# Context stack ahead of staging, routing exponentials behind the tanh, adds a slot later: a cross-attention and expert block on one core

## The reference

```
def layernorm(x): ...                     # mean and variance over the last axis
# cross attention, 16 heads of 64; the rows of the second layernorm are queries
ln = layernorm(layernorm(x)) * g + b      # 512 rows for each batch
xn = layernorm(context) * g + b           # 32 rows for each batch
q, kv = ln @ Wq, concat([xn @ Wkv, ln @ Wkv])
sim  = (rmsnorm(q) * 64**-0.5) @ rmsnorm(k).T   # 512 x 544 for each head; mask on the 32
attn = softmax(sim);  a = (attn @ v) @ Wout + bout
x = x + tanh(g_xattn) * a
# experts: 8, of width 256; all are computed, the two best of each row are kept
p = softmax(layernorm(x) @ router);  w = softmax of the two largest, 0 elsewhere
y = sum over e of w[e] * ((silu(h @ gate[e]) * (h @ up[e])) @ down[e])
x = x + tanh(g_ffn) * y
```

## Time and profile before

| | |
|---|---|
| median of 3 runs | 346.26 us |
| the profiled execution | 347.66 us, its span 345.9 us |
| TensorE busy | 301.0 us, 87% of the span |
| DVE busy | 273.5 us, 79% |
| GpSimd busy | 268.0 us, 78% |
| ScalarE busy | 204.9 us, 59% |
| mean granted TensorE clock | 0.975 |
| DMA engines, mean share | q1 28.8% |

### The profile page before, as it was taken

One profiled execution on the slowest core, in us unless ns is written; L12 is line 12 of the kernel. 1 busy time (PEld: TensorE's weight loads), 2 busy tenths in 40 slices (PEclk: granted clock), 3 DMA queues, 4 the chain that ended last, 5 costly groups with the idle time before them and its releaser, 6 DMA issues.

```text
span 345.9 us, 8714 instructions
## 1 busy us (share of the span) xinstructions
PE 301.0 (87%) x3321; PEld 184.3 (53%) x3321; DVE 273.5 (79%) x515; ACT 204.9 (59%) x357; POOL 268.0 (78%) x203
## 2 busy tenths in 40 slices
PE   0566578789999999999999999999987898988992
PEld 0233243446555555555555656788764674654652
DVE  3898878958899899898988976955647885887994
ACT  2463746727756757665766656467662657554551
POOL 8689896866999999999989987565971475875562
PEclk9996969989999999999999999999999999999999
DMA  6505322810712614416307259450100000001001
GB/s 165 151 1 127 69 35 44 193 39 17 174 45 49 152 36 107 106 23 148 69 20 164 60 154 181 112 165 9 38 2 3 2 1 0 2 3 31 2 0 33
DMA packets 33708, 23.63 MB, mean 68 GB/s; under 512 B 10818, under 2 KB 33154, under 8 KB 33666
## 3 DMA queue, kind: packets, MB, share of 16 engines
q1 hardware_dynamic: 32722, 23.03, 28.8%
q10 hardware_dynamic: 944, 0.04, 0.2%
HBM read 5.87 MB, written 0.52 MB: 18 GB/s over the span
## 4 chain that ended last, share of the span: by engine, by line
PE 53%; POOL 16%; issue 11%; ACT 5%; DVE 5%; SPq 4%; DMA 4%; POOLq 0%; DVEq 0%; ACTq 0%
POOL p_lo L628 9%; PE big L1526 7%; PE big L1527 7%; PE o_ps L1362 5%; PE big L1381 5%; PE o_ps L1356 4%; PE o_ps L1357 4%; DMA pc_st<-pc_lo 3%; PE tv L1369 3%; POOL rms_r L492 3%; PE pj L1333 2%; PE pj L1292 2%; PE pj L1293 1%; PE pj L1294 1%; POOL x_sb L641 1%
## 5 line engine op out<-in xcount | busy, mean ns | idle before, releaser
L593 POOL TENSOR_TENSOR p_lo<-p 128x1024 f16<-128x1024 f32 x64 | 121.8, 1915 | 13.1 <-ACT p L792 13.1
L792 ACT ACTIVATE p<-big 128x1024 f32<-128x1024 f32 x64 | 65.6, 1025 | 48.9 <-PE big L1527 48.8
L991 DVE TENSOR_REDUCE nm_main<-big 128x2 f32<-128x1024 f32 x64 | 78.2, 1222 | 18.1 <-PE big L1381 17.3
L492 POOL TENSOR_TENSOR rms_r<-meansq,power 128x8 f32<-128x8 f32 x32 | 52.3, 1637 | 16.1 <-DVE meansq L965 16.1
L628 POOL TENSOR_TENSOR p_lo<-p,p_lo 128x512 f16<-128x512 f32 x32 | 37.0, 1158 | 25.9 <-ACT p_lo L865 25.9
L1526 PE MATMUL big<-w 128*128 128x512 f16 x128 | 48.8, 381 | 1.9 <-ACT p L792 1.6
L1527 PE MATMUL big<-w 68*128 68x512 f16 x128 | 48.7, 380 | 0.0
L1356 PE MATMUL o_ps<-v,p 128*128 128x65 f16 x512 | 40.7, 194 | 0.0
L1357 PE MATMUL o_ps<-v,p 128*128 128x64 f16 x512 | 40.6, 195 | 0.0
L1356 PEld LDWEIGHTS o_ps<-v,p 128*128 128x128 bf16 x512 | 35.9, 99 | 6.7 <-issue 3.6
L1357 PEld LDWEIGHTS o_ps<-v,p 128*128 128x128 bf16 x512 | 34.4, 98 | 3.2
(11 more groups left out here) (228 smaller groups left out, 715.6 us busy)
## 6 DMA issues: line engine op xcount, KB each, us to landing
w<-hl SPq DMA_DIRECT2D x32, 256.0 KB, 4.2
w<-hl SPq DMA_DIRECT2D x32, 128.0 KB, 3.7
pc_st<-pc_hi SPq DMA_DIRECT2D x64, 32.0 KB, 1.9
pc_st<-pc_lo SPq DMA_DIRECT2D x32, 32.0 KB, 1.9
hl<-n_kernel_gating_EDF_dram SPq DMA_DIRECT2D x1, 1024.0 KB, 6.5
hl<-L_ffn_kernel_up_EDF_dram SPq DMA_DIRECT2D x1, 1024.0 KB, 5.5
o_sb<-in_L_xattn_Wkv_dram SPq DMA_DIRECT2D x2, 384.0 KB, 7.2
x_sb<-in_x_dram SPq DMA_DIRECT2D x2, 256.0 KB, 3.7
```

What stands on the lines that cost most here:

```text
L492: nc.gpsimd.tensor_tensor(rms_r[:, tau % QT, :], meansq[:, tau % QT, :], power[:, 0:8], ALU.pow).then_inc(rr_ok, 1)
L593: nc.gpsimd.tensor_tensor(p_lo[m % NP][:, :], p[m % NP][:, :], p_hi[m % NP], ALU.subtract).then_inc(plo_ok, 1)
L792: nc.scalar.activation(p[n % NP][:, :], st_ps, ACT.Exp).then_inc(exp_ok, 1)
L991: nc.vector.tensor_reduce(nm_main[:, u % 2, 2 * c:2 * c + 2, q], s2_ps.rearrange("p (k n) -> p k n", k=2), AX_X, ALU.max, negate=True).the ...
```

## The change

- `W_AT`: the staging of unit 1 is issued in slot 2 rather than slot 0, so behind the stack of unit 0, which is issued in slot 1.
- ScalarE: in slot 1 the context exponentials come ahead of the exponential of slot 2, not behind it.
- GpSimd: `pc_lo` of unit 0 is made at the end of slot 1, not in slot 2 behind that slot's p_lo.
- The second entry's row scale: DVE in slot 2 rather than 0, ScalarE's four activations in slot 3 rather than 2.
- Experts: `route_exp` is issued a slot later, behind the tanh and ahead of the cast. GpSimd's add of `ys` is a slot later. Expert 2 is weighted by DVE, not ScalarE; counts of the semaphores follow (`weighted`).
- Output: the second batch goes out in two transfers of two row tiles each.

```diff
--- before.py
+++ after.py
@@ -226,7 +226,7 @@
         qk_at = {8 * u - 20 + 2 * t: QT * u + t for u in range(2, UNITS) for t in range(QT)}
         t_at = {8 * u - 18 + 2 * t: QT * u + t for u in range(2, UNITS) for t in range(QT)}
         v_at = {16 * w - 13 + 4 * t: QT * w + t for w in range(1, UNITS // 2) for t in range(QT)}
-        W_AT = {8 * u - 8 if u else FIRST: u for u in range(UNITS)}
+        W_AT = {(FIRST, 2)[u] if u < 2 else 8 * u - 8: u for u in range(UNITS)}
         cs_at = {8 * u - 4: u for u in range(UNITS)}
 
         LN1_AT = 2
@@ -351,8 +351,14 @@
                 return rt_ps[:, 5].rearrange("p t e -> p (t e)")[:, k * QT:(k + 1) * QT]
             return rs[b][:, k, :]
 
+        BY_ACT = (0, 4, 6)
+
         def weighted_by_dve(e):
-            return e % 2 == 1
+            return e not in BY_ACT
+
+        def weighted(e):
+
+            return len([k for k in range(e + 1) if weighted_by_dve(k) == weighted_by_dve(e)])
 
         block = ctx.enter_context(nc.Block())
 
@@ -453,13 +459,13 @@
             for n in range(FIRST, LAST):
                 slot(n)
             out_v = out.rearrange("b (t p) d -> p (b t) d", p=P)
-            for half in range(B):
-                if half == 0:
-                    sp.wait_ge(yp_ok, E)
-                else:
-                    sp.wait_ge(y_ok, E * QT)
-                sp.dma_start(out_v[:, half * QT:(half + 1) * QT, :], x1[:, half * QT:(half + 1) * QT, :]).then_inc(out_ok, 16)
-            sp.wait_ge(out_ok, 16 * B)
+            sp.wait_ge(yp_ok, E)
+            sp.dma_start(out_v[:, 0:QT, :], x1[:, 0:QT, :]).then_inc(out_ok, 16)
+
+            for first in (QT, QT + 2):
+                sp.wait_ge(y_ok, (E - 2) * QT + first + 2)
+                sp.dma_start(out_v[:, first:first + 2, :], x1[:, first:first + 2, :]).then_inc(out_ok, 16)
+            sp.wait_ge(out_ok, 16 * 3)
 
         @block.gpsimd
         def _(pool):
@@ -595,7 +601,7 @@
                 if n == 1:
 
                     inverse_rms(qk_at[0])
-                if n == 2 or n > 2 and n - 1 in cst_at:
+                if n - 1 in cst_at:
                     u = n // 8
                     pool.wait_ge(cexp_ok, u + 1)
 
@@ -628,20 +634,17 @@
                     nc.gpsimd.tensor_tensor(hid_lo[m % NH], hid[m % NH], hid_hi[m % NH], ALU.subtract).then_inc(hlo_ok, 1)
                 if n == Z_X - 1:
                     second_scale(1)
-                m = n - 3
+                m = n - 4
                 if is_xslot(m) and m % FC == FC - 1 and expert_of(m)[1] == 0:
                     e = expert_of(m)[0]
-                    if weighted_by_dve(e):
-                        pool.wait_ge(ysd_ok, e // 2 + 1)
-                    else:
-                        pool.wait_ge(ysa_ok, e // 2 + 1)
+                    pool.wait_ge(ysd_ok if weighted_by_dve(e) else ysa_ok, weighted(e))
                     if e == 0:
                         pool.wait_ge(x1_ok, QT)
                     need(pool, yp_ok, e)
                     nc.gpsimd.tensor_tensor(x1[:, 0:QT, :], x1[:, 0:QT, :], ys[e % 2].rearrange("p (t d) -> p t d", t=QT),
                                             ALU.add).then_inc(yp_ok, 1)
 
-            for n in range(XSLOTS + 4):
+            for n in range(XSLOTS + 5):
                 expert_slot(n)
 
         @block.scalar
@@ -794,8 +797,8 @@
             def slot(n):
                 if is_slot(n) and n - 1 not in AHEAD:
                     exponentials(n)
-                if n in AHEAD:
-                    exponentials(n + 1)
+                if n == 0:
+                    exponentials(1)
                 if n - 1 in cst_at:
                     u = cst_at[n - 1]
                     act.wait_ge(cst_ok, u + 1)
@@ -806,6 +809,8 @@
                     nc.scalar.activation(pc_hi[:, :], o_ps[0][:, :], ACT.Exp, bias=mask_c[:, batch(u):batch(u) + 1])
                     nc.scalar.activation(pc[:, :], o_ps[0][:, :], ACT.Exp,
                                          bias=mask_c[:, batch(u):batch(u) + 1]).then_inc(cexp_ok, 1)
+                if n == 1:
+                    exponentials(2)
                 if n in qk_at and n > FIRST:
                     squared(qk_at[n])
                 if n in t_at:
@@ -817,7 +822,7 @@
                     need(act, pv_ok, 16 * (w - 1))
                     nc.scalar.activation(V[w % 2][:, t, :, 0:DH], tv[:, :].rearrange("p (h d) -> p h d", d=DH), ACT.Copy,
                                          scale=V_SCALE).then_inc(vhi_ok, 1)
-                if n == LN1_AT:
+                if n == LN1_AT + 1:
                     act.wait_ge(ln1b_ok, 1)
                     for t in range(QT, T):
                         nc.scalar.activation(z[:, t, :], x_sb[:, t, :], ACT.Identity, scale=ln_s[:, t:t + 1],
@@ -858,6 +863,12 @@
                         act.wait_ge(pv_ok, SLOTS - NP + n + 1)
                     need(act, hlo_ok, n + 1 - NH)
                     nc.scalar.activation(hid[n % NH], scores[n % 2][:, 0:512], ACT.Tanh, scale=0.5).then_inc(th_ok, 1)
+
+                for b, at in enumerate((ROUTE_X0, ROUTE_X1)):
+                    if n - 1 in at and 0 in at[n - 1]:
+                        route_exp(b, 0)
+                    if n - 1 in at and 5 in at[n - 1]:
+                        route_exp(b, 1)
                 m = n - 1
                 if is_xslot(m):
                     act.wait_ge(hid_ok, m + 1)
@@ -881,11 +892,6 @@
                         last = nc.scalar.activation(ys[e % 2][:, k * D:(k + 1) * D], o_ps[e % 2][:, k * D:(k + 1) * D],
                                                     ACT.Copy, scale=w_tok[:, k, e:e + 1])
                     last.then_inc(ysa_ok, 1)
-                for b, at in enumerate((ROUTE_X0, ROUTE_X1)):
-                    if n in at and 0 in at[n]:
-                        route_exp(b, 0)
-                    if n in at and 5 in at[n]:
-                        route_exp(b, 1)
 
             for n in range(XSLOTS + 4):
                 expert_slot(n)
@@ -1198,7 +1204,7 @@
                                                    in0=st_ps[0:BC, :].rearrange("p (h d) -> p h d", d=DH),
                                                    scalar=V_SCALE, in1=vc[:, :, 0:DH], op0=ALU.mult,
                                                    op1=ALU.subtract).then_inc(cvlo_ok, 1)
-                if n == 0:
+                if n == LN1_AT:
                     second_entry_scale()
                 if n in S_MORE:
                     maximum(S_MORE[n])
@@ -1623,10 +1629,7 @@
                 if c == 0:
 
                     if 2 <= i < E + 2:
-                        if weighted_by_dve(i - 2):
-                            pe.wait_ge(ysd_ok, (i - 2) // 2 + 1)
-                        else:
-                            pe.wait_ge(ysa_ok, (i - 2) // 2 + 1)
+                        pe.wait_ge(ysd_ok if weighted_by_dve(i - 2) else ysa_ok, weighted(i - 2))
                     need(pe, y_ok, QT * (i - 1 - E))
                     if i == 0:
                         pe.wait_ge(o_ok, HG * UNITS)
```

## The result

The changed kernel takes 344.63 us, the median of 20 runs (341.34 to 346.62), against 346.61 us before (20 runs, 345.55 to 348.14): ratio 0.9938, 95% interval 0.9921 to 0.9954. It is 2 us faster where 4.6 were forecast, and its runs spread over 5.3 us, twice as wide as before.

What follows compares the result with a forecast made beforehand. TensorE was taken to bound attention (busy 124.98 of 125 us), with at most 6.1 us idle in the first half of the expert stage. 2.4 + 1.8 + 0.4 = 4.6 us off the median of 346.26 gave 341.7 us, range 340.2 to 344.4.

Steps and rivals of the forecast that it cites:

- A: Early attention slots: with the stack ahead of staging, TensorE gains 2.4 us (1.6 to 2.8), limited by staging landing at 80.65.
- This holds whether or not the clock recovers: Slots 6 and 7: late staging limits the gain to 2.4 us, with a new wait of about 1.4 us, whatever the clock.
- my own 3.8 us: Slot 6: TensorE could be 3.8 us early, from stall 1.9, slow clock 1.6 and row scale 0.3.
- B: Expert stage: moved exponentials, adds and weighting of expert 2 gain 1.8 us (0.75 to about 2.5).
- TensorE runs without a pause from there: Expert stage after slot 17: TensorE has no further waits, with p_lo 16 and down 16 1.8 us early.
- it isn't added by itself: Slot 15: moving the adds removes a 1.38 us TensorE stall, but DVE is the limit, so no separate gain is counted.
- C: Output in two parts: the last transfer moves half the data, gaining 0.4 us (-0.4 to 0.5).
- The rival of the clock: Slot 7: the clock falls in the new wait, costing 1.6 us; total gain 3.0, time 343.3 us; chance 0.08.
- the rival of a stack that isn't sooner: SyncE's queue waits for pc_lo as before, no gain in front; total gain 2.2, time 344.1 us; chance 0.06.

Runs made afterwards that it cites:

- half-filled run: The changed kernel with 7 matmuls of unused product added in slot 7 ahead of the value projection: 342.72 us.
- back alone: The changed kernel with the edits of slots 0 to 3 undone, expert and output edits kept: 343.5 us, ratio 0.9908.
- old order: The changed kernel with the staging of unit 1 back in slot 0, ahead of the stack: 343.61 us, ratio 0.9914.
- front alone: The kernel before with only the edits of slots 0 to 3: 347.2 us, ratio 1.0019.
- first filled run: The changed kernel with 14 matmuls of unused product added in slot 7 ahead of the value projection, first of two measurements: 342.87 us.

## Why the prediction was wrong

**A, 2.4 us forecast, 1.1 us lost: the step that failed.** Up to slot 6 all steps held: pc_lo at 63.8 (64.1), no stall in slot 3, clock 1.00, the staging's first issue at 70.66 (70.45), a wait of ScalarE in slot 6. What failed is the sentence "This holds whether or not the clock recovers", with the size of the wait under it.
- The landing. I took 10.2 us from first issue to last landing, inside bounds of 9.9 to 11.0; it was 81.73 - 70.66 = 11.1. The trace of the kernel before could have told: there the last issue, at 65.20, was the one that took 4.9 us, so the staging took 11.1 us in all, and "the landing of the very last need not be the longest" was wrong in the very rows it was taken from. TensorE took up the projection at 83.42 instead of 84.70; less the 0.3 us by which this execution began sooner, 1.0 us was left instead of 2.4.
- The wait. The slots up to 6 came up as worked out: ScalarE was free for the high halves at 78.67 (81.73 less 3.06), 4.3 us before its 82.93 of the kernel before, or 4.0 less the same 0.3, for 3.8. TensorE kept 1.0 of these 4.0 us, so its wait was 3.0 us, not 1.4; nearly all of the difference is the later landing.
- The clock. From the projection to the first gate-up it is 173.72 us before (84.70 to 258.42) and 175.86 after (83.42 to 259.28): 2.1 us more, from the stretch at 0.50. I had the fall as a rival, priced at what it had cost before (1.6 us) and given 0.08. It came, and dearer, in the profile. The error lay in weighing it by a wait of 1.4 us, like the harmless 1.48 us at 63.66, where a stall of 3 us was what my own 3.8 us and a late landing gave.

The Trainium skill (TensorE: Matmul & The Clock Gate, "HAM oscillation — how this bites in real kernels") says that waits for transfers between bursts of matmuls can put the clock back to its half level each time. The trace agrees at 83.42 (0.50 behind 3.01 us) and at 72.3 before. The section quoted in the prediction ("A second HAM failure mode: psum-queue depth-cycling") is on frequent short idles between groups of matmuls, and the single idle of 1.46 us in the half-filled run was followed by no fall (clock 1.00).

**B, 1.8 us forecast, 3.4 measured** (2.7 in the one profile of the changed kernel, whose last slots are slow). Counted from the first gate-up, gate 13 is 1.26 us sooner (1.25 forecast), gate 17 2.4 (2.05), p_lo 16 2.0 (1.8), and gate 20 still 1.9; so far the working holds. From gate 22 to the end it is 3.4. Mis-sized is the last sentence, "TensorE runs without a pause from there": the kernel before has a stall of 1.57 us at 315.56, for the add of expert 7, which the move of the adds removes as well. I had followed it through slot 18 only. So "it isn't added by itself" was wrong in size too: the adds' slot is the largest of the three edits (2.0 us when undone, read at the gates from slot 22 on, which leaves out the slow last slots), then the routing exponentials (1.0) and expert 2 (0.8). These sum to 3.8, over the 3.4 of all at once, so they overlap.

**C, 0.4 us forecast, 0.5 measured**, as argued: the data time halves. The Trainium skill (DMA: Bandwidth & Descriptors, "Anatomy of one DMA") gives a fixed cost near 2.0 us, in a section on transfers that GpSimd issues. These are issued by SyncE, and 128 KB landed in 1.8 us, under that figure; 2.3 and 1.8 us for 256 and 128 KB leave 1.3 us that don't depend on the size (an estimate from the two).

With the front at its measured worth (0.6 us lost by the times) and the back at its own (3.2 of 346.6 us by the ratio), the sum is 2.6 us; 2.1 came. A was too high by 3.5 us and B too low by 1.6, so the second error hid part of the first. The rival of the clock, 343.3, named the mechanism but not its size, and it took the staging as in at 80.65. That the rival of a stack that isn't sooner, 344.1, is the nearest number is luck: the stack was sooner. Why single executions of the changed kernel differ by 5.3 us is shown in part: in the profile the clock fell, and over the executions the time goes with the mean clock (339.3 us of span at 0.981, 344.6 at 0.958). Another part lies ahead of the slots: the first turned scores start anywhere from 53.8 to 55.9 us in the 14 profiles, and no edit touches what is ahead of them.

## What to carry to other kernels

Where a reordered queue removes one wait and makes another, price the new wait by how early everybody else will then be, not by how late the old order was, and give a long one the price of the slow clock behind it: here the wait cost 3.1 us and the clock nearly as much again in the profiled execution, half of that in the medians. A queue need not be reordered as a block: only what is due first has to go first, and two heads of four turned a loss into 4.5 us. And follow an engine that "runs without a pause" to the end of its rows before saying so.

## What the runs showed that I had not expected

- The value of work that is thrown away: 7 matmuls of 512 columns in an idle of 3 us made attention 2.8 us shorter in the profile, and the kernel 1.9 us faster by the medians (1.5 by the ratios).
- Which waits of TensorE in the first slots were followed by the half clock: 1.84 us (back alone), 1.91 (before), 2.26 (old order), 3.01 (changed) and 3.51 us (front alone) were; 1.02, 1.46 and 1.48 us were not. The kernel before already lost by one of these. A long wait is not the only way to it: the first filled run was slow from 60.0 to 63.4 us with nothing over 0.72 us ahead.
- How exactly a stage repeats: the expert stage is 80.17 to 80.21 us in seven of the nine profiles with all of its edits (80.8 in the other two, where the clock fell ahead of the last adds), where whole executions spread by 1 us and often 2 or more. Edits of under 1 us can be read there, and not in the times.
